# GpSimd's program order in a cross-attention and mixture-of-experts kernel: weight splits behind their own loads, values and bias additions in other places

## What is computed

```python
x = x + attention(layernorm(x), ctx, ctx)      # 16 heads of 8, projections 128x128
x = x + ffn(layernorm(x))
# ffn, for all 2048 tokens:
logits = gelu(xf @ w_r1 + b_r1) @ w_r2 + b_r2  # router over 8 experts, best 2 kept
for _ in range(2):
    ctx = concat([integrated, v])              # 256 wide
    shared = gelu(ctx @ w_s1 + b_s1) @ w_s2 + b_s2
    ctrl   = gelu(ctx @ expert_w1[i] + b1) @ expert_w2[i] + b2   # the 2 chosen experts
    x_next, v_next = weighted mix of the shared and the routed update
    halt = sigmoid(gelu(x_next @ w_h1 + b_h1) @ w_h2 + b_h2)
    integrated += halt * (gelu(x_next @ w_f1 + b_f1) @ w_f2 + b_f2) * integration_weight
    v = v_next
```

## Time and profile before

| what | us |
|---|---|
| three runs | 386.26, 386.38, 389.85 |
| median | 386.38 |
| profiled execution, device time | 388.05 |
| its span, first to last instruction | 385.8 |
| TensorE busy in it | 342.6 (89%) |
| VectorE busy | 285.8 (74%) |
| ScalarE busy | 273.8 (71%) |
| GpSimd busy | 30.1 (8%) |
| mean granted TensorE clock | 0.966 of full speed |

### The profile page before, as it was taken

How to read it: one execution, slowest core, us unless ns; L and a number is a source line. 1 busy time by engine, 2 the same in 40 slices (tenths; PEclk the granted TensorE clock), 3 DMA queues, 4 the chain that set the end, 5 groups by cost and what they waited for, 6 DMA issues and landing times. The chain is left out here.

```text
span 385.8 us, 5578 instructions
## 1 busy us (share of the span) xinstructions
PE 342.6 (89%) x1663; PEld 220.3 (57%) x1663; DVE 285.8 (74%) x620; ACT 273.8 (71%) x444; POOL 30.1 (8%) x43
## 2 busy tenths in 40 slices
PE   4969699888988878997987998999999999999975
PEld 2435344434433356675564765776776786786743
DVE  7776966857624587589999897894995996798752
ACT  6642366586685789894958856896897997797812
POOL 9007731001000000000000000000000000000000
PEclk9976699999989999999999999999999999999988
DMA  4360000000000000000000000000000000001000
GB/s 117 92 168 3 3 1 5 0 1 6 3 3 0 1 3 2 1 0 2 1 0 1 2 0 2 1 0 0 3 0 0 3 0 27 3 0 29 1 28 27
DMA packets 10748, 5.15 MB, mean 13 GB/s; under 512 B 4355, under 2 KB 10655, under 8 KB 10719
## 3 DMA queue, kind: packets, MB, share of 16 engines
q1 hardware_dynamic: 10719, 4.81, 4.6%
HBM read 3.62 MB, written 1.05 MB: 12 GB/s over the span
## 5 line engine op out<-in xcount | busy, mean ns | idle before, releaser
L701 PE MATMUL bank<-qs,w_hi 128*128 128x512 f32 x160 | 65.6, 410 | 0.6 <-ACT qs L1017 0.5
L702 PE MATMUL bank<-qs,w_lo 128*128 128x512 f32 x160 | 62.4, 390 | 0.0
L884 ACT ACT_TABLE_LOAD x45 | 57.7, 1283 | 1.6 <-PEq L1393 0.7
L961 ACT ACTIVATE PT<-bank 77x512 f32<-77x512 f32 x64 | 35.3, 589 | 20.9 <-PE bank L812 14.1
L706 PE MATMUL bank<-KB,w_hi 128*128 128x512 f32 x160 | 42.8, 389 | 0.0
L1002 ACT ACTIVATE hid<-bank,cols 128x512 f32<-128x512 f32 (+1 forms) x48 | 31.4, 683 | 13.1 <-PE bank L668 12.5
L1281 DVE SCALAR_TENSOR_TENSOR masked<-Ib,cst,hid 128x512 f32<-128x512 bf16 x32 | 23.4, 751 | 20.9 <-ACT hid L1002 20.7
L701 PEld LDWEIGHTS bank<-qs,w_hi 128*128 128x128 f32 x160 | 30.1, 188 | 9.7 <-issue 2.0
L702 PEld LDWEIGHTS bank<-qs,w_lo 128*128 128x128 f32 x160 | 30.0, 188 | 7.7 <-issue 1.7
L706 PEld LDWEIGHTS bank<-KB,w_hi 128*128 128x128 f32 x160 | 30.0, 188 | 6.4
L823 PE MATMUL bank<-PT,VO 128*32 128x512 f32 x256 | 31.8, 598 | 0.4 <-ACT PT L961 0.4
(11 more groups left out here) (234 smaller groups left out, 662.2 us busy)
## 6 DMA issues: line engine op xcount, KB each, us to landing
x_tok<-in_x_dram SPq DMA_DIRECT2D x4, 256.0 KB, 3.4
out_dram<-x_tok SPq DMA_DIRECT2D x3, 256.0 KB, 2.3
hid<-in_L_ffn_expert_w_dram SPq DMA_DIRECT2D x1, 576.0 KB
masked<-in_L_ffn_expert_w_dram SPq DMA_DIRECT2D x2, 192.0 KB
wf_sb<-in_L_ffn_w_f_dram SPq DMA_DIRECT2D x2, 128.0 KB
qs<-mT SPq DMA_DIRECT2D x16, 8.0 KB
out_dram<-x_tok SPq DMA_DIRECT2D x2, 128.0 KB, 1.8
hid<-in_L_ffn_expert_w_dram SPq DMA_DIRECT2D x2, 96.0 KB
```

What stands on the lines that cost most here:

```text
L701: pe.matmul(t[:], lhsT=w2_hi[:, tile_of(k - 1, j), o:o + D], rhs=hi, start=(j == 0), stop=False)
L702: pe.matmul(t[:], lhsT=w2_lo[:, tile_of(k - 1, j), o:o + D], rhs=hi, start=False, stop=False)
L884: act.add_instruction(mybir.InstLoadActFuncSet(name=nc.get_next_instruction_name(), act_func_set_id=chosen, ins=[], outs=[]))
L961: step(act.activation(PT[0:KL, i % PT_TILES, :], ST[i % SCORE_BANKS][0:KL, :], ACT.Exp, scale=float(DH) ** -0.5))
```

## The change

The 30 weight loads are counted on three semaphores: 10 loads of first-layer expert weights on `moe1_in`, 7 of the second layer on `moe2_in`, 13 others on `ffnw_in`. The loads themselves, their order and their queue stay. `w1split` waits for `moe1_in` and for `ln1x` of batch 1 on VectorE; `w2split` waits for `moe2_in`; its three small operations become a stage of their own, `w2rest`, which waits for `ln1x` of batch 2. The two places in which TensorE and ScalarE waited for `w2split` wait for `w2rest`. The table numbers of GpSimd's stages are new.

```diff
-    return {"xbo": 1, "w1split": 2, "w2split": 5, "ones": NG, "vput": NG}.get(stage, 0)
+    return {"xbo": 1, "w1split": 2, "w2split": 2, "w2rest": 3, "ones": NG, "vput": NG}.get(stage, 0)
...
-    "setup2": ((None, 11.9, 22.84, None), 0), "w2split": ((None, None, None, -45.54), 0),
-    "w1split": ((None, None, None, -108.88), 0),
+    "setup2": ((None, 11.9, 22.84, None), 0), "w2split": ((None, None, None, -80.0), 0), "w2rest": ((None, None, None, -75), 0),
+    "w1split": ((None, None, None, -95.0), 0),
...
-        N_VEC, N_ATT, N_CTX, N_PROJ, N_FFN = 12, 5, 1, 5, 30
+        N_VEC, N_ATT, N_CTX, N_PROJ, N_FFN, N_MOE1, N_MOE2 = 12, 5, 1, 5, 13, 10, 7
...
                 if stage == "w1split":
-                    pool.wait_ge(ffnw_in, 16 * N_FFN)
+                    pool.wait_ge(moe1_in, 16 * N_MOE1)
+                    pool.wait_ge(dve_done, dve_at("ln1x", 1))
...
                 elif stage == "w2split":
-                    pool.wait_ge(ffnw_in, 16 * N_FFN)
+                    pool.wait_ge(moe2_in, 16 * N_MOE2)
                     step(pool.tensor_copy(w2_hi[:], w2_in))
                     pool.wait_ge(pool_done, n[0])
                     step(pool.tensor_tensor(w2_lo[:], w2_in, w2_hi[:].bitcast(F32), ALU.subtract))
-                    pool.wait_ge(pool_done, n[0])
+                elif stage == "w2rest":
+                    pool.wait_ge(pool_done, pool_at("w2split", 0))
+                    pool.wait_ge(dve_done, dve_at("ln1x", 2))
...
                     if n == 0:
-                        pe.wait_ge(pool_done, pool_at("w2split", 0))
+                        pe.wait_ge(pool_done, pool_at("w2rest", 0))
...
                     else:
-                        act.wait_ge(pool_done, pool_at("w2split", 0))
+                        act.wait_ge(pool_done, pool_at("w2rest", 0))
```

More of the change, by code:

```diff
@@ L128 @@
 SETUP = {
-    "ones": ((None, None, None, -15.68), 0), "clear": ((None, None, -69.2, None), 0), "wka": ((None, -93.87, None, None), 0),
+    "ones": ((None, None, None, -100.0), 0), "clear": ((None, None, -69.2, None), 0), "wka": ((None, -93.87, None, None), 0),
     "vecs": ((-4.72, -4.26, None, None), 0), "prep": ((None, None, -54.11, None), 0), "cols": ((-48.05, -34.22, None, None), 0),
@@ L458, in xattn_moe_kernel @@
         CT = [[bank[4], bank[5], bank[3]], [bank[6], bank[7], bank[2]]]
-        const_in, vec_in, attw_in, ctx_in, proj_in, ffnw_in = (
-            sem(n) for n in ("const_in", "vec_in", "attw_in", "ctx_in", "proj_in", "ffnw_in"))
+        const_in, vec_in, attw_in, ctx_in, proj_in, ffnw_in, moe1_in, moe2_in = (
+            sem(n) for n in ("const_in", "vec_in", "attw_in", "ctx_in", "proj_in", "ffnw_in", "moe1_in", "moe2_in"))
         x_in = [sem(f"x_in{b}") for b in range(B)]
@@ L560, in _ @@
                 each = e_w1.rearrange("e (f c) h -> f c e h", f=2)[f]
-                load(w1_in[:, f, 1:NK].rearrange("c j (e h) -> c (j e) h", e=2), each[:, 1:E - 1], ffnw_in)
-                load(w1_in[:, f, 0, 0:H], each[:, 0], ffnw_in)
-                load(w1_in[:, f, 0, H:P], each[:, E - 1], ffnw_in)
+                load(w1_in[:, f, 1:NK].rearrange("c j (e h) -> c (j e) h", e=2), each[:, 1:E - 1], moe1_in)
+                load(w1_in[:, f, 0, 0:H], each[:, 0], moe1_in)
+                load(w1_in[:, f, 0, H:P], each[:, E - 1], moe1_in)
                 for r in range(2):
[L565 to L570, removed]
+                    load(w1_in[:, f, NK, r * H:(r + 1) * H], w_s1.rearrange("(f c) h -> f c h", f=2)[f], moe1_in)
+            load(w2_in[:, 1:NK], e_w2[1:E - 1].rearrange("(k e) h o -> (e h) k o", e=2), moe2_in)
+            load(w2_in[H:P, HIGH], e_w2[E - 1], moe2_in)
+            load(w2_in[0:H, LOW], e_w2[0], moe2_in)
+            load(w2_in[0:E, HIGH], e_b2, moe2_in)
+            load(w2_in[H:H + E, LOW], e_b2, moe2_in)
             for r in range(2):
-                load(w2_in[r * H:(r + 1) * H, NK], w_s2, ffnw_in)
+                load(w2_in[r * H:(r + 1) * H, NK], w_s2, moe2_in)
             load(wf1_sb[:], w_f1, ffnw_in)
```

6 lines of the change are left out of this document (3 added, 3 removed).

## The result

The changed kernel takes 384.38 us, the median of 20 runs (383.06 to 390.46). The kernel before takes 388.62 us in the 20 runs beside it (386.26 to 391.36). The ratio is 0.9905 with a 95% interval of 0.9882 to 0.9929, so the change saves 0.95%, about 3.7 us (2.8 to 4.6). The two medians lie 4.2 us apart. A run more than 1.5% above the fastest of its kernel (390.46 us here, 388.22 in the repeat of the change, 393.44 among the values behind the additions) counts as slow and stands in no ratio; with it the means here would differ by 3.4 us instead of 3.7. The three runs shown with the kernel before, median 386.38, were at its low end. That the absolute forecast of 384.1 us came out nearly exact is luck: its start was 2.2 us too low and the gain of 2.3 us behind it was too small.

A forecast was written before the change was run, and what follows sets the result against it. It took GpSimd's long subtraction holding a small VectorE instruction near 40.8 us as the stall: up to 2.48 us, limited to 2.3 by `qs`, other terms nothing, so 386.38 - 2.3 = 384.1 us, range 382.3 to 386.6.

The forecast's parts named there:

- What bounds the kernel: GpSimd, 8% busy, matters only where others wait: its second-layer subtraction holds VectorE's TENSOR_SCALAR at 40.78 for 2649 ns.
- The splits start earlier: GpSimd's first cast at 27.2 instead of 30.64, second subtraction over at 40.1; worth nothing or up to 2.48 us.
- The margin of 0.7 us: Room between the second subtraction's end at 40.1 and VectorE's TENSOR_SCALAR due at 40.78; late loads eat it first.
- What is late next: Behind the freed TENSOR_SCALAR, `qs` waits for ScalarE's `taken` and starts at 41.85, not 44.12; 2.3 us remain, `sc` at 44.2.
- Rests, additions, ones: GpSimd's small rests and bias additions end at 52.7, costing nothing or 1.3 us; early memsets of ones nothing to 0.45.
- Values: Batch 0's values on GpSimd move to 32 us so `pv` need not wait for them; no gain of their own.
- The sum: Whole kernel: 2.3 us saved, 388.05 to 385.75 us in the profiled execution, 386.38 to 384.1 us at the median.
- up to 2649 - 170 ns = 2.48 us: Most that earlier splits could bring: the held TENSOR_SCALAR near 40.8 us falling back to its usual length.
- A: Rival, chance 0.22: low clock still comes at 41.9 and lasts to 48.7; net gain 1.15, 385.2 us.
- D: Rival, chance 0.14: clock stays high from 35 on, low stretch of 113.5 to 117.0 goes too; 382.4 us.
- B: Rival, chance 0.06: low clock from 41.9 lasts 10.4 us, to 52.3; loses 2.95 against 2.3 gained, 387.0 us.
- C: Rival, chance 0.08: late loads or hand-overs let the splits still meet the TENSOR_SCALAR; full loss gives 386.4 us.

The follow-up runs named there:

- the repeat of the change: The changed kernel, nothing altered, run again on one chip beside three shifts of it: 384.42 us, ratio 0.9876 to the kernel before.
- the values behind the additions: The changed kernel with the values of batches 0 and 1 moved behind the bias additions of batches 0 to 2: 390.65 us, ratio 1.0027.
- all loads waited for: The changed kernel, but its first split waits again for all 30 loads, as before: 389.29 us, ratio 0.9993.
- ones in the gap: The kernel before with ten products of ones added on TensorE in the pause behind the stalled TENSOR_SCALAR: 388.48 us, ratio 0.9964.
- without the guard: The changed kernel without the first split's wait for `ln1x` of batch 1: 395.95 us, ratio 1.016.
- the six pieces of 128x384: The kernel before with its second subtraction cut into six pieces at the same place: 386.85 us, ratio 0.9949.

## Why the prediction was right, and where it was off

*What bounds the kernel.* Right. GpSimd matters only where it holds VectorE. Moving one subtraction out of the way gave the full gain, and putting the chain back gave all of it back.

*The splits start earlier.* Right in mechanism: 27.2 forecast for the cast and 26.73 measured, 40.1 for the end of the subtraction and 39.49 measured. The margin of 0.7 us was wrong. It was reckoned against VectorE's arrival at 40.78, which belongs to one execution. In the profile after, the arrival is 39.13 and the margin is -0.4; it costs 0.2. In the repeat it is +0.6, and there the forecast can be read as it was meant: VectorE came at 40.53, `qs` started at 41.59 and the first `sc` products at 43.97, for 41.9 and 44.2 in the forecast.

*What is late next.* In the profile after, `qs` and the first `sc` products came at 40.20 and 42.40, not at 41.9 and 44.2. They were 1.7 and 1.8 us earlier than forecast, for the reason just named. The hand-over behind the stall is as reckoned: 1.07 us from the start of the TENSOR_SCALAR to `qs` both here and in the forecast (41.85 - 40.78).

*Rests, additions, ones.* Right: the additions ended 0.77 us before the next TENSOR_SCALAR, where I had given 0.7. *Values.* Right: no gain of their own, and with the move undone all of the gain is gone (390.65 us).

*The sum.* The mechanism is right and the size is off: the term "up to 2649 - 170 ns = 2.48 us", of which 2.3 were taken, comes from one profiled execution and stood for what the stall is worth in every one. The hold ended at 43.43 us in the profile of before, and at 43.03 and 43.28 in the two variants that keep its chain (all loads waited for, ones in the gap). It began at 40.78, 38.75 and 38.75, and so took 2.65, 4.28 and 4.53 us. The start follows the clock: over the 13 profiles other than that without the guard, VectorE came at 40.53 to 40.98 in the three in which the first low stretch lasted to about 35, and at 38.75 to 39.24 in the ten in which it ended between 29.5 and 31.7. With the old chain a VectorE that comes sooner waits just that much longer. So the change brings 2.3 us in the one case, and 2.27 + 1.62 = 3.9 or 2.27 + 1.89 = 4.2 in the other, by the table. The measured gain within the span, about 3.3, lies between. How often the kernel before is in which case isn't known, as there is one profile of it; the other 0.4 us lie outside the span, and the sum had no term for them.

The clock gives a second account, from the runs with their times alone. 63 runs of the kernel before have a mean of 389.1 us at a mean granted clock of 0.9655, and 24 of the change 384.9 at 0.9739. Among runs at nearly the same clock, 0.974 to 0.975, the kernel before has 386.8 us (7 runs) and the change 384.4 (9 runs): 2.3 us of the 4.2, of which 0.4 lie outside the span, while the rest goes with a clock that is higher on average. The two accounts can't be added. An early rise does not make a high mean clock by itself: with all loads waited for the clock rose early (29.5), the hold took 4.28 us, the low stretch behind it lasted to 50.0, and the mean clock was 0.960 at 390.50 us, lower and slower than the profile of before with its late rise (0.966 and 388.05 us). So part of the difference in clock may itself come from the longer hold. How the gain parts between them stays open.

*The rivals.* The clock pattern of A (low from 41.5 to 48.3) was there in the repeat, and that of D (high there and at 113.5) in the profile after, with another low stretch at 92. Neither is a property of the change; both are executions of one kernel. In the repeat A's mechanism took back 0.67 us, where 1.15 had been reckoned, and D's missing stretch at 113.5 gave 0.98, where up to 1.7 had been. The rows have the first low stretch start at 24.8 and not at 24.6, so B's 10.4 us should be 10.2, which changes nothing. B, the slower case, was seen in no profile. C was half there: the splits still touch the TENSOR_SCALAR, for 0.2 us.

## What to carry to other kernels

An instruction that is ten times its usual length is a wait that no view of waits names; look for it by the greatest duration against the median of its group, and for the instruction of the other engine that ends with it. A stall has two ends. Find out, from a second execution or from what releases each side, which of them is pinned: the other one moves from execution to execution, and the stall is worth as much as it is long on average, not as much as one profile shows. Compare the device time with the span too, since a difference between two kernels can lie outside the span. An engine with little to do is best moved to where its neighbour does nothing that it can hold, and earlier is not better by itself: without its guard the same change costs 1.6% against the kernel before.

## What the runs showed of the hardware that I had not expected

A hold can last across more than one GpSimd instruction in a row. In the repeat of the change a TENSOR_SCALAR took 2.81 us, across the ends of two memsets, and without the guard one took 2.30, across the last copies and the cast. But often one slips through: at 5.25 us in the kernel before it took 1.12, to the end of the first memset alone; between two of the six pieces of 128x384 it took 0.17; and without the guard one took 0.34 at the turn from the cast to the subtraction. What decides between the two is not shown.

The TENSOR_TENSOR of 128x4 with both inputs in SBUF was held beside the subtractions (1.21 us beside the first one without the guard, 0.85 beside the pieces of the second, for 0.16). BATCH_NORM_STATS2 kept its length beside the second one (0.86 for four, before), and so did TENSOR_REDUCE from PSUM (0.47, beside the pieces).

The granted clock differs from execution to execution of one kernel. Among the runs of the changed kernel a mean of 0.983 went with 383.1 to 383.5 us and one of 0.961 with 388.5 to 388.6. This spread is larger than the effect of the change, and a prediction from one profile stands on one draw of it.
